# Distance attention of a decoder: query and key copies move to ScalarE and GpSimd, small steps are dropped or reordered

## The reference

```
B, D, H = 8, 128, 16
DH = D // H

scores = jnp.einsum('bhid,bhjd->bhij', qh, kh) / jnp.sqrt(jnp.float32(DH))
s_ = jnp.where(maskb, scores, -1e+32)
p = jax.nn.softmax(s_, axis=-1) * maskb.astype(scores.dtype)
cum = jnp.cumsum(p, axis=-1)
tot = jnp.sum(p, axis=-1, keepdims=True)
pos = jnp.abs(idx[None, :] - idx[:, None])
dist_scores = jnp.sqrt(jnp.clip((tot - cum) * pos, 0.0, None))
gamma = -jax.nn.softplus(gammas)[None]
diff = jnp.exp(jax.nn.sigmoid(pdiff))[:, None]
total_effect = jnp.clip(jnp.exp(dist_scores * gamma * diff), 1e-05, 100000.0)
scores = scores * total_effect
scores = jnp.where(maskb, scores, -1e+32)
scores = jax.nn.softmax(scores, axis=-1)
scores = scores.at[:, :, 0, :].set(0.0)
return jnp.einsum('bhij,bhjd->bhid', scores, vh)
```

## Time and profile before

| | us |
|---|---|
| median of 3 runs (1295.37 to 1296.4) | 1296.01 |
| the profiled execution | 1292.0 |
| its span in the profile | 1290.2 |
| PE busy (share of the span) | 898.0 (70%) |
| DVE busy | 970.7 (75%) |
| ACT busy | 639.5 (50%) |
| POOL busy | 249.2 (19%) |
| DVE busy between 118 and 251 us | 129.91 of 133.00 |

### The profile page before, as it was taken

How to read it: one execution, slowest core, us unless ns; L and a number is a source line. 1 busy time by engine, 2 the same in 40 slices (tenths; PEclk the granted TensorE clock), 3 DMA queues, 4 the chain that set the end, 5 groups by cost and what they waited for, 6 DMA issues and landing times. The chain is left out here.

```text
span 1290.2 us, 18553 instructions
## 1 busy us (share of the span) xinstructions
PE 898.0 (70%) x6172; PEld 589.7 (46%) x6172; DVE 970.7 (75%) x2502; ACT 639.5 (50%) x1418; POOL 249.2 (19%) x383
## 2 busy tenths in 40 slices
PE   5957676576875304245997959889978625999977
PEld 2533334333543104134884624666645314666654
DVE  5899999935665798997356864888868497898833
ACT  4767878713442405055224723787447421566632
POOL 1330000001000000000012220389522022332101
PEclk9985555567997656577999978899979867999978
DMA  6000000001546001010100000000000000000000
GB/s 215 2 1 0 1 1 1 1 17 65 122 111 152 3 1 68 1 68 34 34 1 1 2 1 0 1 2 1 2 1 1 1 0 1 1 2 2 1 1 16
DMA packets 26623, 30.12 MB, mean 23 GB/s; under 512 B 1185, under 2 KB 23073, under 8 KB 25506
## 3 DMA queue, kind: packets, MB, share of 16 engines
q1 hardware_dynamic: 26530, 28.95, 8.1%
HBM read 19.50 MB, written 9.44 MB: 22 GB/s over the span
## 5 line engine op out<-in xcount | busy, mean ns | idle before, releaser
L2070 PEld LDWEIGHTS l2a_b_ps<-l2a_diag,l2a_uT 128*128 128x128 f32 x512 | 64.9, 194 | 29.1 <-issue 16.6
L2070 PE MATMUL l2a_b_ps<-l2a_diag,l2a_uT 128*128 128x128 f32 x512 | 69.3, 280 | 6.4 <-DVE l2a_convh L2281 5.4
L2804 PE MATMUL l1w_mem_ps<-l1a_rows,l1w_post 128*128 128x64 f32 x16 | 4.7, 390 | 95.6 <-DVE l1a_rows L2946 95.6
L2832 ACT ACTIVATE l1w_score<-l1w_mix_ps 128x264 f32<-128x264 f32 (+7 forms) x29 | 12.0, 451 | 109.3 <-DVE l1a_rows L2946 92.6
L2919 DVE MATCH_REPLACE8 l1w_minus<-l1w_low,l1w_minus 128x129 f32<-128x129 f32 (+39 forms) x264 | 64.5, 262 | 0.0
L2794 PE MATMUL l1w_mix_ps<-l1a_rows,l1w_pre 128*128 128x264 f32 (+7 forms) x58 | 30.3, 693 | 43.7 <-DMA l1a_rows<-scores_dram 25.3
L2913 DVE MAX8 l1w_low<-l1w_minus 128x8 f32<-128x129 f32 (+37 forms) x332 | 59.6, 259 | 0.4
L2777 POOL TENSOR_SCALAR_AFFINE_SELECT l1w_score<-l1w_score 128x256 f32<-128x256 f32 x8 | 4.1, 506 | 245.4 <-ACT l1w_score L2832 245.4
L2804 PEld LDWEIGHTS l1w_mem_ps<-l1a_rows,l1w_post 128*128 128x128 f32 x16 | 4.3, 307 | 100.5 <-DVE l1a_rows L2946 99.3
L623 ACT ACTIVATE l3a_l3x_probT<-l3a_l3x_turn_ps 128x512 f32<-128x512 f32 x64 | 38.1, 596 | 23.5 <-PE l3a_l3x_turn_ps L500 22.8
L500 PE MATMUL l3a_l3x_turn_ps<-pack,l3a_l3x_prob 128*128 128x128 f32 x256 | 41.6, 287 | 10.3 <-ACT l3a_l3x_probT L623 5.7
(11 more groups left out here) (588 smaller groups left out, 2837.4 us busy)
## 6 DMA issues: line engine op xcount, KB each, us to landing
scores_dram<-l1p_dots SPq DMA_DIRECT2D x8, 924.0 KB, 7.1
l1a_rows<-scores_dram SPq DMA_DIRECT2D x5, 1056.0 KB, 5.0
l1a_rows<-scores_dram SPq DMA_DIRECT2D x24, 132.0 KB, 3.6
scores_dram<-l1p_dots SPq DMA_DIRECT2D x8, 132.0 KB, 3.6
pack<-in_pack SPq DMA_DIRECT2D x1, 761.5 KB, 9.7
pack<-in_pack SPq DMA_DIRECT2D x2, 321.5 KB, 6.7
pack<-in_pack SPq DMA_DIRECT2D x1, 612.0 KB, 11.6
pack<-in_pack SPq DMA_DIRECT2D x1, 576.0 KB, 10.6
```

The source lines that it names most:

```text
L2070: mm = nc.tensor.matmul(bx_ps(n)[:, j * S:(j + 1) * S], uT[:, c, b, :], diag[:, s % 2, b, :], start=True, stop=True)
```

## The change

For sequences 2 to 7 ACT copies the query and the key (`copy_qk` in `scalar`, behind `copy_sums`), and POOL spreads the key (`spread_keys`). DVE keeps the copies of sequences 0 and 1. The rate is made of two instructions and a reciprocal, in place of three, and gamma is stored as the reciprocal of its square, for which turn 0 of the self attention gets one instruction more. ACT roots the grid before both halves of the sums, and the rate before the second half. `divide` loses its second instruction. The products are made in two calls, and `dve_scale` stands between them. On PE the mask matmuls are a step of their own (`mark`), of which the first stands ahead of `transpose_sums`, and `transpose_norm` moves ahead of the second `weigh`.

```diff
@@ class Distances @@
+            dve.wait_ge(self.gamma_set, 2)
+            nc.vector.reciprocal(self.inv_gamma2[:], self.inv_gamma2[:]).then_inc(self.gamma_set, 1)
+
+FIRST = 2
@@ DistanceAttention, pool @@
+        def spread_keys(b):
+            pool.wait_ge(qk_set, b + 1)
+            after(pool, scores_mm, 2 * (b - 1))
+            pool.tensor_tensor(km[b % 2][:], bcast_mid(k_flat[:], HH), bcast_last(cm.col("head4"), S),
+                               ALU.mult).then_inc(km_set, 1)
+
         def rest():
-            for b in range(B):
-                ln.pool_store(pool, cm, b)
+            for now in range(1, B + 2):
+                if now >= 2:
+                    ln.pool_store(pool, cm, now - 2)
+                if FIRST <= now + 1 < B:
+                    spread_keys(now + 1)
@@ tensor @@
+        def mark(b, half):
+            after(pe, scaled_set, 2 * (b - 1) + half + 1)
+            for g in (2 * half, 2 * half + 1):
+                nc.tensor.matmul(bank(g), cm.ident_bf[:], bcast_mid(cm.masks[mask], HH), start=True, stop=False)
+
         def score(b, half):
             pe.wait_ge(qk_set, b + 1)
-            after(pe, scaled_set, 2 * (b - 1) + half + 1)
...
-            for g in pair:
-                nc.tensor.matmul(bank(g), cm.ident_bf[:], bcast_mid(cm.masks[mask], HH), start=True, stop=False)
-            for g in pair:
+            if b >= FIRST:
+                pe.wait_ge(km_set, b - FIRST + 1)
+            for g in (2 * half, 2 * half + 1):
...
-                    weigh(now - 1, 1)
-                    transpose_sums(now - 1)
                 if inside(now - 2):
                     transpose_norm(now - 2)
+                if inside(now - 1):
+                    weigh(now - 1, 1)
+                if inside(now + 1):
+                    mark(now + 1, 0)
+                if inside(now - 1):
+                    transpose_sums(now - 1)
                 if inside(now + 1):
                     score(now + 1, 0)
+                    mark(now + 1, 1)
                     score(now + 1, 1)
@@ scalar @@
+        def copy_qk(b):
+            act.wait_ge(qk_mm, b + 1)
+            after(act, scores_mm, 2 * (b - 1))
+            after(act, km_set, b - FIRST)
+            nc.scalar.activation(q[b % 2][:], qk_ps[:, 0, :], ACT.Identity, bias=w("bq"))
+            nc.scalar.activation(k_flat[:], qk_ps[:, 1, :], ACT.Identity, bias=w("bk")).then_inc(qk_set, 1)
...
                     load_root_table()
+                    root_grid(now)
                     root(now, 0)
                 if inside(now - 1):
                     copy_probT(now - 1, 0, 1)
                 if inside(now):
+                    root_rate(now)
                     root(now, 1)
-                    root_grid(now)
-                    root_rate(now)
                     load_exponential_table()
...
                     copy_sums(now - 1)
+                if FIRST <= now + 1 < B:
+                    copy_qk(now + 1)
@@ vector @@
-            nc.vector.tensor_scalar(rate[:], left[:, :, :, 0], 1e-18, None, ALU.max).then_inc(rate_set, 1)
-            dve.wait_ge(rate_set, 3 * b + 1)
+            for half in range(2):
+                last = nc.vector.scalar_tensor_tensor(out=rate[:, half, :], in0=left[:, half, :, 0], scalar=1e-18,
+                                                      in1=inv_gamma2[:, HALF * half:HALF * half + HALF],
+                                                      op0=ALU.max, op1=ALU.mult)
+            last.then_inc(rate_set, 1)
+            dve.wait_ge(rate_set, 2 * b + 1)
             nc.vector.reciprocal(rate[:], rate[:]).then_inc(rate_set, 1)
-            dve.wait_ge(rate_set, 3 * b + 2)
-            nc.vector.tensor_tensor(every(rate), every(rate), gamma2[:], ALU.mult).then_inc(rate_set, 1)
...
-            dve.wait_ge(recip_set, 2 * b + 1)
-            nc.vector.tensor_scalar(rz[:], rz[:], cm.col("not_first"), None, ALU.mult).then_inc(recip_set, 1)
-            dve.wait_ge(recip_set, 2 * b + 2)
+            dve.wait_ge(recip_set, b + 1)
...
                 if inside(now):
-                    products(now)
-                if inside(now + 1) and now:
-                    copy_qk(now + 1)
+                    products(now, 0)
                 if inside(now - 2):
                     ln.dve_scale(dve, nc, cm, now - 2)
                 if inside(now):
+                    products(now, 1)
                     second_scores(now)
```

46 lines of the change are left out of this document (26 added, 20 removed).

## The result

| | before | after |
|---|---|---|
| median of the runs made together (4 each) | 1296.2 | 1287.06 (1285.71 to 1288.49) |
| profiled execution, span | 1292.0, 1290.2 | 1286.86, 1285.0 |
| DVE busy | 970.7 | 963.6 |
| POOL busy | 249.2 | 266.6 |
| first scan to last division of the distance stage | 188.3 | 180.9 |

The ratio is 0.9928, 95% interval 0.9902 to 0.9955. The last line of the table is worked out from two starts, that of the first scan (L1366) and that of the last division (L1410).

The account below looks back on a forecast made before the run. DVE bounds the distance stage. Six turns at 0.71 give 4.26, plus 0.24 (turns 0 and 1), 0.26 (turn 7) and 0.27 (tail): 5.0 us off the 1296.0 median, 1291.0 us; range 1287.3 to 1294.3.

Parts of the forecast that it names:

- P: Zero point of a distance-stage turn: DVE has given out the last product and takes the next instruction.
- the middle between its two bounds: Rate on DVE: two independent steps and a reciprocal save between 0 and 0.20 us a turn; 0.10 taken.
- the 0.20 charged: Turn 1: ACT's second root, its table and its copies come later, charged at 0.20 us.
- the sum: Whole kernel: savings of six turns, turns 0 and 1, turn 7 and the tail, together 5.0 us.
- nothing in the rows supports PE at its upper level there: Distance stage: PE's granted clock stays at 0.50, 1.2 GHz, so a half of the score products takes 2.08 us.
- full saving: Rival: earlier key or faster scores remove the stalls before the maxima; 8.5 us saved, 1287.5 us, chance 0.13.
- the second maximum hangs on PE's work at the lower clock: Argument against vanishing stalls: 2.97 + 2.08 us of PE work before the second maximum, which no reordering shortens.
- Eaten by the scores: Rival: masks, transposes and key queue, first score product at P + 3.9 to 4.2; 1293.5 to 1295.5 us, chance 0.15.
- the rate's root, no stall in the ordinary turn: Ordinary turn: ACT has some 0.90 us of DVE's statistics for the rate's root of 0.20, so no stall.
- The slower rival: POOL's key spreading waits until the second maxima are through; turn 24.0 us, kernel 1305.4 us, chance 0.05.
- single products of 0.27 leave gaps to POOL: Products: DVE's single instructions of 0.27 us leave port gaps, so POOL's step keeps its normal 0.55.
- The row waits for POOL: Rival: products hold POOL's two steps, DVE waits about 1.0 us a turn between halves; 1297.0 us, chance 0.03.

Follow-up runs that it names:

- r_after2: The kernel after the change, unmodified, run a third time: median 1284.86 us, ratio 0.9918 to the kernel before.
- r_after: The kernel after the change, unmodified, run again: median 1283.47 us, ratio 0.9911 to the kernel before.
- r_before: The kernel before the change, unmodified, run again: median 1295.28 us, ratio 1.0006.
- w_keep: The kernel after, with spare identity matmuls in PE's idle times in the distance stage: median 1282.87 us, ratio 0.9895 to the kernel before.
- a_delay: The kernel after, with six 128x1024 fills on DVE before the second scores of turn 4: median 1291.58 us, ratio 0.9971 to the kernel before.
- b_pad: The kernel before, with nineteen one-column fills at the start of DVE's program: median 1291.98 us, ratio 0.9975.
- b_copies: The kernel before, with only the query and key copies moved to ACT, POOL spreading the key and PE waiting for it: median 1293.79 us, ratio 0.9986.
- b_mark: The kernel before, with only the masks split off on PE and the first pair moved ahead of the transposes: median 1299.80 us, ratio 1.0023.
- a_root: The kernel after, with the roots of grid and rate back behind the second root: median 1285.36 us, ratio 0.9923 to the kernel before.
- best1: The kernel after, with copies, spreading and scores moved earlier and the division behind the next products: median 1285.77 us, ratio 0.9934 to the kernel before.
- b_copiesroot: The kernel before, with the query and key copies moved and the roots of grid and rate ahead of the second root: median 1293.60 us, ratio 0.9989.
- a_peold: The kernel after, with PE's old order, masks and scores behind the transposes: median 1286.14 us, ratio 0.9920 to the kernel before.
- b_pad8: The kernel before, with eight one-column fills at the start of DVE's program: median 1291.04 us, ratio 0.9954.

## Why the prediction was right and wrong

**Right: what bounds the stage, and the new turn up to the rate.** From P = 182.98 the first score product starts at P + 3.46 (forecast 3.48), the first maximum at P + 5.57 (5.61), the second at P + 8.56 (8.58), the scans at P + 11.16 (11.18), the rate at P + 15.70 (15.71). The spreading takes 1.04 in all six turns. The rate's root of turn 1 lets the products start 0.59 earlier than before, against 0.61. The stall of 0.15 before the first maximum is some 0.07.

**Sizes that were off.** The rate takes 0.44 (198.68 to 199.12), where the step took the middle between its two bounds, 0.50; the pair of independent tiny steps takes 0.27 from start to start (198.68 to 198.95), where one step took 0.21 before (179.06 to 179.27). The statistics take 0.81 and not 0.90. Together with smaller remainders a steady turn is 21.40 and not 21.58: 6 x 0.18 = 1.1. On the other side turn 1 costs more than the 0.20 charged. There ACT's new work delays the effect and the key, DVE has idle times of 0.22 and 0.33 besides the usual one (r_after2), and that turn is 22.00. Turns 0 and 1 up to P of turn 1 give 0.79 where 0.44 was forecast; the reciprocal of gamma, charged at 0.27, lies ahead of the stage (at 33.34 in the first profile) in front of an idle time in which DVE waits for PE. From P of turn 7 on it is 0.45 for 0.53. The six turns between give 4.39 for 4.06: turn 1 gives only 0.03 where 0.51 was forecast, the other five 0.87 each for 0.71. By r_after2, where the clock did not rise, the stage thus gains 5.6 for the 5.0 of the sum, and the error of 0.6 is that of the sum proper.

**Wrong: the clock of the stage.** The step that failed is the sentence that nothing in the rows supports PE at its upper level there; the sum takes all its PE work at 0.50. The rival "full saving" named the mechanism, with turns of 21.0, and it came true in three turns of the first profile, in one of r_after and in none of r_after2: worth 1.8, 0.5 and 0. What the step lacked is that the granted clock differs from run to run, that only the traces with the whole change have a rise in these turns, and that DVE there waits for PE, so that a faster PE counts. r_before has a rise as well, between 108 and 114 us, and its turn there is 22.73, the same as in the first profile of that kernel without it. w_keep shows the rest: with the clock up in most turns, the turn is 20.94. That rival's argument that the second maximum hangs on PE's work at the lower clock did not hold either: a_delay has a turn of 20.98 at 0.50, with the key early. Its number, 1287.5, lies near the 1287.06 measured, but by luck: in the profile of r_after2 the clock never rises in these turns and the stage gives 5.6, and its median is still 10.7 under the kernel before.

**Wrong: that the rest of the kernel stays as it was.** This is the larger error, and the one that put the measurement outside the range. The sum put the stage's saving on the median of the whole, with no term for what lies outside the stage. Nobody reads 1000 us of untouched code for a change of 20 lines, and no row in the prediction speaks of it. Yet the last attention and what follows it are 5.4 shorter in all three profiles of the kernel after. b_pad gives 3.6 (1.2 to 5.2) by the medians without the change. The sum, 3.6 for this and 5.6 for the stage, is 9.2; with the 5.4 of the profiles it is 11.0. Measured were 9.1 at first and 11.7 and 10.7 in the repeats, and the intervals of all of them take in both sums, so the close match of 9.2 and 9.1 says little.

**The parts together.** "Eaten by the scores" did not come true, but b_copies and b_mark show that it was near: 22.63 and 22.76. What the prediction said of the rate's root, no stall in the ordinary turn, held, but its reason, that the statistics leave ACT time, is not enough by itself: it needs the new order of the roots. The prediction credited the earlier roots with turn 1 only. With the roots in the old order, in a_root, the loss is 0.59 in every ordinary turn. The slower rival, the spreading held by DVE, did not come true where the change put it. best1 brought it about, by moving the spreading beside a scan. POOL's store of the row (L203) is held: it takes 2.19 in the kernel after, where it lies beside products with two SBUF inputs, and 0.29 in the kernel before and in b_copies; nothing waits for it. The prediction's remark that single products of 0.27 leave gaps to POOL is true of its one-column steps beside them (0.28 and 0.55), not of this store. "The row waits for POOL" did not come: no idle time stands before L185.

**What stays open.** Why DVE has an idle time of 0.30 at one row with nothing waited for, and by which rule it moves with the stream, is not settled; that the one at L718 hangs on DVE's stream, not on POOL's, PE's or ACT's nor on the time of the start, is. Nor is it shown that this idle time makes the clock fall some 100 us later: all five traces with it have the fall, but b_copies has no idle time at L718 and a fall all the same (158.1), and b_copiesroot, with the same DVE stream, has neither (154.7). Another pattern goes with the idle times at l2a_hs: in the three kernels where one is 1.1 or more (a_peold, b_pad8, b_copies), and in no other, the clock in the first 8 us of the last attention is 0.71, elsewhere 0.74 or 0.75. Nor was it taken apart what in the change lets the clock rise in the stage. The kernel's runs also scatter by 2 to 4 us for reasons that lie outside the stage.

## What to carry to other kernels

When work leaves the bounding engine, write down the chain that will deliver to it next, and check that no unconditional part of the receiving step (here the masks) stands behind the new wait: the copies and the masks are each a loss alone. Look as well for the engine that has no idle time to give behind the one that is delayed (here ACT's roots). Place a POOL instruction that reads SBUF beside DVE work with an operand in PSUM, not beside a scan, even if that means later. And before a few us are credited to a change, look at untouched stages in both traces: here a third to a half of the difference came with a granted clock far away, which a few idle fills on one engine also bring.

## What the runs showed of the hardware

- The granted clock of TensorE rose or not in the same turn of one kernel, from run to run: the same score products took 2.08 or 1.13.
- Spare matmuls brought the mean clock of the stage from 0.50 to 0.78 at equal busy time.
- Nineteen one-column fills at DVE's start made the kernel 3.6 us shorter (0.9975, 0.9960 to 0.9991); on POOL they did not (1.0018, 0.9999 to 1.0037).
- Two DVE steps of 128x8 took 0.90 instead of 0.24 while a POOL instruction of 2.13 held the port, and a POOL copy took 2.19 instead of 0.29 beside DVE's products.
